# Segment sum of 100,000 edges in a graph layer: accumulating scatters replaced by a counting sort, plain scatters and one-hot products

## What is computed

```python
xn = layernorm(x)
edge_proj = edge_attr @ W_sum + b_sum            # 100000 x 128 by 128 x 256
sum3d = segment_sum(edge_proj, src, 6250)        # the part that the change is about
gnn = xn + z_in[in_deg] + z_out[out_deg] + sigmoid(cent) + sigmoid(vor) + sum3d
x = x + gnn + linear_attention(xn)               # "mix"
x = x + moe_ffn(layernorm(x))                    # 8 experts, top 2, hidden 1024
```

## Time and profile before

| what | us |
|---|---|
| runs of the kernel | 2334.79, 2337.32, 2340.21 (median 2337.32) |
| span of the profiled execution | 2335.5 |
| POOL busy in the 782 accumulating scatters | 1258.5 |
| last of these scatters starts at | 1541.6 |
| last stretch (FFN) begins at about | 1741 |

### The profile page before, as it was taken

How to read it: one execution, slowest core, us unless ns; L and a number is a source line. 1 busy time by engine, 2 the same in 40 slices (tenths; PEclk the granted TensorE clock), 3 DMA queues, 4 the chain that set the end, 5 groups by cost and what they waited for, 6 DMA issues and landing times.

```text
span 2335.5 us, 38410 instructions
## 1 busy us (share of the span) xinstructions
PE 1721.3 (74%) x12869; PEld 1379.6 (59%) x12869; DVE 1450.0 (62%) x3795; ACT 728.8 (31%) x1607; POOL 1545.5 (66%) x1009
## 2 busy tenths in 40 slices
PE   2555545477778777767777677349479999999998
PEld 1333334344445444556666566249378888888887
DVE  2789978777787777233333332139966666666665
ACT  1011111144444444211111111127344444444442
POOL 2888888888888888888888888830023455444442
PEclk9676655579999999778888888669689999999999
DMA  9987777765454445555555555456618989999995
GB/s 304 231 177 176 144 144 159 151 112 69 69 76 70 69 70 70 76 72 86 74 82 75 81 75 75 44 117 201 200 30 253 268 266 276 274 267 278 270 269 159
DMA packets 401456, 348.02 MB, mean 149 GB/s; under 512 B 39303, under 2 KB 323530, under 8 KB 401260
## 3 DMA queue, kind: packets, MB, share of 16 engines
q1 hardware_dynamic: 268492, 266.72, 36.5%
q0 software_dynamic: 132768, 78.84, 29.2%
HBM read 236.69 MB, written 108.76 MB: 148 GB/s over the span
## 4 chain that ended last, share of the span: by engine, by line
PE 35%; POOL 24%; DMA 18%; issue 14%; DVE 7%; ACT 1%; POOLq 0%; SPq 0%; DVEq 0%; ACTq 0%
POOL node_table L1535 24%; DMA node_table<-edge_sums,row_i 18%; PE bank L730 12%; PE bank L744 12%; PE bank L687 2%; DVE hotB L871 2%; PE bank L607 1%; PE bank L482 1%; PE bank L716 1%; PE bank L699 1%; PE bank L701 1%; DVE hotA L868 1%; PE bank L679 1%; PE bank L663 1%; PE bank L672 1%
## 5 line engine op out<-in xcount | busy, mean ns | idle before, releaser
L1535 POOL DMA_INDIRECT node_table<-edge_sums,row_i x782 | 1258.5, 1609 | 278.8 <-issue 207.6
L1333 ACT COPY edge_sums<-bank 128x387 f32<-128x387 f32 (+1 forms) x261 | 125.2, 480 | 1055.1 <-DMA node_table<-edge_sums,row_i 801.8
L482 PE MATMUL bank<-edge_rows,same_node 128*128 128x129 f32 x1564 | 289.9, 333 | 208.7 <-issue 108.0
L482 PEld LDWEIGHTS bank<-edge_rows,same_node 128*128 128x128 f32 x1564 | 248.0, 236 | 254.0 <-issue 230.6
L1561 POOL DMA_INDIRECT result<-mixw,edge_rows x105 | 168.2, 1602 | 283.7 <-DVE mixw L1290 198.4
L1487 ACT ACTIVATE mixw<-bank,edge_rows 128x256 f32<-128x256 f32 (+1 forms) x456 | 243.2, 548 | 328.4 <-PE bank L730 212.7
L730 PE MATMUL bank<-edge_rows,big 128*128 128x256 f16 (+1 forms) x2736 | 290.9, 265 | 4.6 <-ACT mixw L1487 2.3
L744 PE MATMUL bank<-big 128*128 128x256 f16 x2520 | 284.4, 273 | 1.0 <-issue 1.0
L730 PEld LDWEIGHTS bank<-edge_rows,big 128*128 128x128 f16 x2736 | 250.0, 98 | 37.5 <-ACT mixw L1487 3.1
L504 PE MATMUL bank<-hotA,hotB 128*128 128x49 bf16 x1564 | 116.6, 200 | 198.6 <-DVE hotB L871 190.2
L744 PEld LDWEIGHTS bank<-big 128*128 128x128 f16 x2520 | 244.2, 98 | 28.5 <-issue 1.3
(11 more groups left out here) (283 smaller groups left out, 2515.3 us busy)
## 6 DMA issues: line engine op xcount, KB each, us to landing
big<-w_parts SPq DMA_DIRECT2D x114, 1024.0 KB
edge_rows<-edge_attr SPq DMA_DIRECT2D x130, 384.0 KB
big<-L_ffn_W SPq DMA_DIRECT2D x128, 128.0 KB
w_parts<-big SPq DMA_DIRECT2D x64, 256.0 KB
node_table<-z_parts SPq DMA_DIRECT2D x20, 640.0 KB, 7.4
node_table<-edge_sums,row_i POOLq DMA_INDIRECT x782
mixw<-node_table SPq DMA_DIRECT2D x96, 128.0 KB, 2.4
edge_rows<-L_ffn_b SPq DMA_DIRECT2D x57, 128.0 KB
```

The source lines that it names most:

```text
L482: ins = e.matmul(ps_sum[:, i * XW:(i + 1) * XW], S[:, g % SRING, i * P:(i + 1) * P], X[:, c // LOAD % XRING, c % LOAD, :], start=True, sto ...
L1535: e.indirect_dma_start(table[t], bass.IndirectOffsetOnAxis(ap=row_i[:, g % ORING, i:i + 1], axis=0), O[:, g % ORING, i, 0:RW], None, compu ...
```

## The change

The edge rows are no longer added in DRAM. The program finds for each edge its place in the order by node tile (a counting sort over 50 tiles, in four parts of 60, 300, 280 and 142 columns), writes the raw rows with their node number as a 129th value to that place with a plain indirect DMA, reads the sorted rows back in blocks of 256, and sums each block with one-hot products into an accumulator in SBUF (128 x 50 x 128, transposed). A block that holds rows of more than one tile is visited once for each tile: 588 visits in 147 batches of 4. The tables, their zeroing, the matching of equal nodes and the loads of the tables are gone. The degree steps now take 10 columns, and all numbers for one-hots are stored twice side by side, so that the innermost axis of each operand is two adjacent bf16 values. There are 312 ticks, two for each load of 5 columns. The counting of the first 6 chunks and then of all 79 comes ahead of tick 0. In the side steps, ACT's second normalization of `state` is dropped (an identity matrix is added into `mq` instead), and the rest stage turns `xn` again instead of keeping it.

```diff
-GROUP = 3
-LOAD = 6
-TABLES = 4
-START = 8
-TICKS = GROUPS + 5
-DEGREES = 3.6
+LOAD, XRING = 5, 5
+CHUNK = 2 * LOAD
+PART_ENDS = (6, 36, 64, CHUNKS)
+VROWS, VB = 2, 4
+X2RING = 3
+TICKS = 2 * LOADS
+START = 14
+SIDE_AT = ((START, 0), (96, W_TICK0 + W_TICKS), (176, FOLD0), (TICKS - 16, SIDE_STEPS))
+DEGREE_AT = ((START, 0), (136, 2 * CHUNKS + 2))
+VISIT_TICKS = ((100, 0), (4 * PART_ENDS[1], VISIT_AT[1] // VB), (4 * PART_ENDS[2], VISIT_AT[2] // VB),
+               (TICKS, VISIT_AT[3] // VB))
...
+    def tensor_rank(e, k):
...
+        e.matmul(ps_rank_hot[:, 0:w], rankm, sort_hot[:, n % 2, 0:w], start=True, stop=False).then_inc(hot_used, 1)
+        row = identh[:, k:k + 1].to_broadcast([P, P])
+        e.matmul(ps_rank_hot[:, 0:w], row, base_hi[:, 0:w], start=False, stop=False)
+        e.matmul(ps_rank_hot[:, 0:w], row, base_lo[:, 0:w], start=False, stop=True).then_inc(ranked, 1)
...
+    def tensor_visit(e, v):
+        b = v - 3
...
+        for i in range(VB):
+            for k in range(VROWS):
+                ins = e.matmul(ps_visit[b % 2][:, i * P:(i + 1) * P], visit_rows[:, b % X2RING, i, k, 0:EDIM],
+                               visit_hot[:, b % 2, i, k, :], start=(k == 0), stop=(k == VROWS - 1))
+        ins.then_inc(visit_summed, 1)
...
+    def one_hots(out, n, width, values, c0):
+        half = width // 2
+        return (out.rearrange("p (a b r) -> p a b r", a=n, r=2),
+                iotab[:, 0:width].rearrange("p (b r) -> p b r", r=2).unsqueeze(1).to_broadcast([P, n, half, 2]),
+                values[:, c0:c0 + n, :].unsqueeze(2).to_broadcast([P, n, half, 2]))
...
+    def vector_rank(e, k):
...
+        e.reduce_max(sort_top[:, k % 2, 0:n], ps_rank_hot[:, 0:n * SORT].rearrange("p (j g) -> p j g", j=n), AX.X).then_inc(rank_read, 1)
+        e.wait_ge(rank_read, k + 1)
+        e.tensor_scalar(row_pos[:, c0:c0 + n], sort_top[:, k % 2, 0:n], float(PART_FIRST[q] * CHUNK * P) - BIG, None,
+                        ALU.add).then_inc(pos_made, 1)
...
+    def vector_visit(e, v, regs):
+        b = v - 4
+        if 0 <= b < BATCHES:
+            e.load(regs, visit_i[OFF_ROW:OFF_ROW + 1, VB * b:VB * (b + 1)])
+            e.wait_ge(visit_summed, b + 1)
+            for i in range(VB):
...
+                e.tensor_tensor(acc[:, bass.ds(o, P)], acc[:, bass.ds(o, P)], ps_visit[b % 2][:, i * P:(i + 1) * P],
+                                ALU.add).then_inc(acc_added, 1)
+        b = v - 2
+        if 0 <= b < BATCHES:
+            e.wait_ge(visit_loaded[b % X2RING], 16 * VB * (b // X2RING + 1))
...
+            e.tensor_tensor(visit_hot[:, b % 2].rearrange("p v k n -> p (v k) n"), iota.unsqueeze(1).to_broadcast([P, n, P]),
+                            visit_key[:, b % 2].rearrange("p v k -> p (v k)").unsqueeze(2).to_broadcast([P, n, P]),
+                            ALU.is_equal).then_inc(visit_hot_made, 1)
...
+    def scalar_key(e, n):
...
+        x_free(e, n)
+        e.copy(X[:, n % XRING, :, EDIM:XW], src_f[:, c:c + LOAD].unsqueeze(2)).then_inc(keyed, 1)
...
     def scalar_edges(e, tick):
...
+        n, i = divmod(tick, 2)
+        if i == 0 and n >= 2:
+            scalar_key(e, n + XRING - 2)
...
-                e.indirect_dma_start(table[t], bass.IndirectOffsetOnAxis(ap=row_i[:, g % ORING, i:i + 1], axis=0),
-                                     O[:, g % ORING, i, 0:RW], None, compute_op=ALU.add, bounds_check=ROWS - 1,
-                                     oob_is_err=True).then_inc(table_added[t], 16)
...
+    def pool_scatter(e, c, rows, done):
+        e.indirect_dma_start(sorted_rows, bass.IndirectOffsetOnAxis(ap=row_pos[:, c:c + 1], axis=0), rows, None,
+                             bounds_check=ETILES * P - 1, oob_is_err=True).then_inc(done, 16)
...
+    def sync_visit(e, b):
...
+        for q in range(PARTS):
+            if b == VISIT_AT[q] // VB:
+                part_sorted(e, q)
+        if b >= X2RING:
+            e.wait_ge(visit_summed, b - X2RING + 1)
+        for i in range(VB):
+            n = VB * b + i
+            at_ = e.value_load(visit_i[BLOCK_ROW:BLOCK_ROW + 1, n:n + 1], min_val=0, max_val=sum(PART_BLOCKS) - 1)
+            e.dma_start(visit_rows[:, b % X2RING, i].rearrange("p k w -> p (k w)"),
+                        sorted_blocks[bass.ds(at_, 1)].rearrange("o p n -> p (o n)")).then_inc(visit_loaded[b % X2RING], 16)
```

More of the change, by code:

```diff
@@ L188, in build_layer @@
+    wide = scratch(VMAX)
+    ends_f = scratch(2 * P)
+    ends_i = scratch(2 * P).bitcast(I32)
+    ends_b = scratch(2 * P)
+    taken, visit_n, visit_end, visit_at, visit_skip = (scratch(P) for _ in range(5))
+    passed_v, owner_v = scratch(VMAX), scratch(VMAX)
+    upto = scratch(P)
+    assert at[0] <= TILES * DIM
     edge_mem = X.rearrange("p a b c -> p (a b c)")
@@ new lines, in build_layer, with x_there, x_free, part_sorted @@
+    SMALL_ALL = 16 * (KC * 3 + PAIRS + 5 + 4)
+    def x_there(e, n):
+        e.wait_ge(x_loaded[n % XRING], 16 * (n // XRING + 1))
+    def x_free(e, n):
+        if n >= XRING:
+            e.wait_ge(scattered[n % XRING], 16 * LOAD * (n // XRING))
+    def part_sorted(e, q):
+        n = min(LOADS, 2 * PART_ENDS[q])
+        for r in range(XRING):
+            more = ETILES - LOADS * LOAD if q == PARTS - 1 and r == LOADS % XRING else 0
+            e.wait_ge(scattered[r], 16 * (LOAD * len(range(r, n, XRING)) + more))
@@ L758, in tensor_program @@
                 tensor_rest(e, u)
-        for tick in range(TILES + 13):
+        for v in visit_steps(TICKS):
+            tensor_visit(e, v)
+        for tick in range(TILES + 8):
             tensor_nodes(e, tick)
@@ L1306, in vector_program @@
                 vector_rest(e, u)
-        for tick in range(TILES + 13):
+        for v in visit_steps(TICKS):
+            vector_visit(e, v, regs)
+        for tick in range(TILES + 9):
             vector_nodes(e, tick)
@@ L1490, in scalar_program @@
     def scalar_program(e):
-        scalar_index(e)
+        for n in range(XRING):
+            scalar_key(e, n)
         for tick in range(TICKS):
             scalar_edges(e, tick)
+            for v in visit_steps(tick):
+                scalar_visit(e, v)
             for d in degree_steps(tick):
@@ L1539, in pool_gather, with pool_last_edges @@
+    def pool_last_edges(e):
+        e.wait_ge(x_last, 32)
+        e.wait_ge(keyed, LOADS + 1)
+        e.wait_ge(pos_made, CHUNKS)
+        for c in range(LOADS * LOAD, ETILES):
+            pool_scatter(e, c, XL[:, c - LOADS * LOAD, :], scattered[LOADS % XRING])
     def pool_gather(e, j):
@@ L1565, in pool_program @@
         pool_constants(e)
-        for tick in range(TICKS):
-            pool_edges(e, tick)
+        for n in range(LOADS):
+            pool_edges(e, n)
+        pool_last_edges(e)
         for j in range(XG - 1):
@@ L1820, in sync_program @@
             sync_edges(e, tick)
+            for v in visit_steps(tick):
+                sync_visit(e, v)
             for d in degree_steps(tick):
```

815 lines of the change are left out of this document (447 added, 368 removed).

## The result

The changed kernel took 2501.94 us (median of 4 runs), the kernel before 2336.06 beside it: a ratio of 1.070, 95% interval 1.067 to 1.073. Foretold were 2260 us and a gain. The profiled execution took 2489.35 us, its span 2487.6.

The account below looks back on a forecast made before the run. It took POOL's scatter beat to bound most of the edge stage, then DVE the nodes stage. Edge stages at their slowest engine, 1475 us, plus 98.6 and 683.5, gave 2257, stated as 2260; range 2130 to 2370.

Parts of the forecast that it names:

- the tail: From the last scatter to the nodes stage: landing 4 us, 120 visits on SP 137, last batch 10, start 3; 154 us.
- stage by stage, the slowest engine each time: Edge stage: each stage priced by its slowest engine, 100 + 320 + 385 + 285 + 231 + 154 = 1475 us.
- POOL's beat: Plain scatters on POOL: 1.01 us of work plus 0.30 of issue, 1.31 us, against 1.85 with accumulation.
- rival 2: POOL's plain scatter keeps the accumulating scatter's beat of 1.85 us: 2434 us in all; chance 12%.
- One-hots at half rate: DVE's one-hots with paired bf16 operands: 500 wide take 0.42 us, 1280 wide 0.82.
- Rival 3: DVE's one-hots don't run in pairs and take the full rate: 2410 us in all; chance 10%.
- DVE's register reads: Four registers read from SBUF by DVE before each batch of visits: between nothing and 0.75 us, 0.3 taken.
- the 30 us: Ticks 14 to 96: DMA engines might just fill if the new pair stayed as dear; only the range allowed this.
- SP, 1.14 us a visit: Each of 588 visits costs SP a register read and a DMA, 1.14 us; 4.6 us a batch of four.
- POOL beside DVE: Edge stage: the trace does not bear out that DVE's two-SBUF-input instructions delay POOL's scatters; 1% chance left.
- rival 1: POOL stays the bound in the ticks because the other engines overlap better: about 2035 us; chance 8%.

Follow-up runs that it names:

- e13: The changed kernel unchanged, run again in a later job: 2222.6 us, ratio 0.954 to the kernel before.
- e14: The changed kernel with SP reading a batch's four block numbers in one load of four registers: 2131.9 us, ratio 0.915 to the kernel before.
- e11: The changed kernel with POOL clearing a 320-wide scratch tile after each scatter, beat 1.53 us: 2307.1 us, ratio 0.989 to the kernel before.
- e12: The changed kernel with POOL's 320-wide clear after each scatter and SP's one load of four registers per batch: 2232.7 us, ratio 0.957 to the kernel before.
- e5: The changed kernel unchanged, run once more beside the kernel before: 2510.4 us, ratio 1.075.
- e10: The changed kernel unchanged, run beside two paused variants in one job: 2460.5 us, ratio 1.054 to the kernel before.
- e3: The changed kernel without the visits (block loads, keys, one-hots, products, adds), so edge sums stay zero: 1939.8 us.
- e4: The changed kernel with SP loading the visits' blocks from constant addresses, without the 588 register reads: 2118.4 us.

## Why the prediction was wrong

**Its sum came out within 2% where signals were prompt, in part by luck.** In e13 none was late, and the stages can be set against the working (the first four: DVE's maximum L1032 in ticks 14, 98, 178 and 258; the prediction's points shifted by its own rate for two ticks):

| until | foretold | e13 | first profile |
|---|---|---|---|
| tick 14 | 100 | 114 | 161 |
| tick 98 | 430 | 414 | 506 |
| tick 178 | 812 | 784 | 949 |
| tick 258 | 1098 | 1054 | 1289 |
| last scatter | 1321 | 1270 | 1531 |
| nodes stage begins | 1475 | 1451 | 1715 |
| end (span) | 2257 | 2223 | 2488 |

Against e13 the ticks were priced 51 us too dear up to the last scatter and the tail 27 too cheap, and the two errors hide one another. The first profile loses to e13 47, 45, 73, 70 and 26 us up to the last scatter and 3 in the tail, where POOL is silent; nodes, router and FFN take 772 us in both. That is, it loses where POOL scatters the edges and nowhere else.

**The step that failed** is the sentence that sums "stage by stage, the slowest engine each time". It takes for granted that each engine learns at once when PE is done, as all rows of before have it, and it prices POOL's faster beat as a gain only. The runs showed in its place: at a beat of 1.29 us PE's signals come late, by up to 22.8 us, in four of the seven jobs of the changed kernel and its variants; engines that take turns with PE wait, and a stage takes longer than any engine's work in it. No row of before has that; its beat is 1.85. The size is shown twice: 279 us between the first measurement and e13, across jobs, and 153 us within one job when the pauses are put in. The range's upper end of 2370 held 110 us for dearer DMAs, dearer register reads and some waits for PE. A lesson for the range: the change took POOL and the DMAs that it starts to a rate that no row showed, and the rows then set no bound on what the other engines suffer by it.

The windows tell it for the mix stage, the first of e13, the second of the first profile:

```profile
379.00:785.00 406.00, 342.81 (x2053) 220.31 (x2052) 284.04 (x648) 166.57 (x392) 261.03 (x238) 0.95 0.47 129
```

```profile
450.00:922.00 472.00, 352.58 (x1974) 218.42 (x1973) 272.61 (x615) 163.66 (x384) 233.49 (x220) 0.88 0.37 102
```

In e13 PE is busy 84% at a clock share of 0.95, and the 49 tiles take 393 us, about as foretold (47 of them in 385). That agreement is partly luck: the sum had 362 us of work for PE in 385, the window has 343 in 406. In the first profile the 49 tiles take 475 us, with PE 75% busy and its clock at 0.88.

Point by point:
- **POOL's beat** 0.98 + 0.30 = 1.28 us: right (1.31 from the gather), and rival 2's fixed price is out. 521 of the 781 beats of e13 are of this length; others wait or are stretched (see the end). That accumulation is dear by its third descriptor no trace shows.
- **One-hots at half rate**: 500 wide 0.41 us, 1280 wide 0.82: right. Rival 3 did not come.
- **DVE's register reads**: 0.3 was taken; in the first profile and in e13 0.41 us of issue (median) stand ahead of a batch's first add where nothing else ends the wait.
- **DMA bandwidth**: the 30 us weren't needed. Ticks 14 to 98 take 300 us in e13, where 330 were foretold; in the window of 120 to 379 us the DMA engines are busy 0.73.
- **SP, 1.14 us a visit**: right. In e13's tail the visits go at 1.10 to 1.32; PE's 572 products in 160 us are 35.8 batches of 16, 4.47 us each, against 4.6. SP's chain in this tail (L1868 is the DMA's issue, L1867 the read of one register), and the window:

```profile
1300.92 0.34 SPq L1868
1301.30 0.27 SPq L1867
1301.60 0.15 SPq L1867
...
1302.02 0.34 SPq L1868
```

```profile
1280.00:1440.00 160.00, 97.66 (x572) 89.10 (x571) 86.01 (x212) 0.00 (x0) 0.00 (x0) 0.78 0.44 118
```

- **The tail**: 181 us instead of 154. The price was right and the number not: 622 products, 39 batches, come behind the last scatter, not 30: visits of the third part were still to be loaded or in flight. With one read for four numbers (e14) it is 109. Two DMAs of a batch then start 0.53 apart, and DVE is the bound, busy 82% and waited for by PE, as its 3.0 us a batch would have it: 31 batches in 90 us are 2.9 each. SP's chain and the window in e14:

```profile
1299.95 0.33 SPq L1868
...
1300.48 0.33 SPq L1868
...
1301.00 1.11 SPq L1868
```

```profile
1260.00:1350.00 90.00, 63.24 (x495) 57.33 (x494) 73.49 (x186) 0.00 (x0) 0.00 (x0) 1.00 0.67 185
```

- **POOL beside DVE**: "the trace does not bear it out" was misread. In the earlier trace rows a scatter takes 82.67 / 51 = 1.62 us with DVE busy 88.5 of 100, 83.88 / 53 = 1.58 at 80.8 and 83.54 / 55 = 1.52 at 33.4. The last section has what it is worth.
- **Slips in the sums**: 782 x 1.31 is 1024 and not 1028; rival 1 then adds up to 2026, and rival 2 to 2432; 60 pairs and 16 matchings leave 38 us of the 88.5 and not 36; 362 and 268 us at a clock of 0.95 are 381 and 282. None changes the verdict.
- **The chances**: I gave 23% to slower, with two causes, rivals 2 and 3, neither of which came. A mechanism that no row hints at had no chance of its own.

## What to carry to other kernels

A wait that ends long after its producer did, several waiters of one engine let go at the same moment, and a producer whose next instructions run on undisturbed point at a late signal and not at a slow engine. A lacking record alone doesn't: DVE's had no effect here. Count late signals by comparing the raise of the semaphore with the end of the instruction, and lacking records beside them, before pricing anything else. A verdict on a change that raises the rate of POOL's indirect DMAs needs the unchanged partner in the same job, and more than one job; and the cheapest test is a pause behind each DMA. Where addresses for several DMAs lie side by side, read them with one load of several registers: 72 us of tail here from e13 to e14, 76 from e11 to e12, and 91 and 74 us in all.

## What the runs showed that was not expected

- **PE's signals, and not DVE's or ACT's, arrive late** in some jobs while POOL issues indirect DMAs 1.29 us apart: 262 to 289 of 787 to 941 recorded in the first measurement and e5 to e10; 32 of 960 at 1.53; none of 1507 at 1.85 in the kernel before. In e3, e4, e13 and e14 none was late at the same 1.29. The jobs differ in the records that lack; what makes them differ the traces don't show, nor why it is PE.
- **The scatters themselves wait for some of DVE's instructions.** In e13 their median is 0.98 us and their mean 1.12; the excess over 0.98 sums to 113 us. What counts is what DVE is at when the scatter starts. Of 96 that start during the one-hot L1071, whose inputs both lie in SBUF, 76 take over 1.1 us, and all but one of these end 0.85 to 0.86 us after the one-hot. Of 100 that start during the adds L1059, with one input in PSUM, none does; beside an idle DVE 1 of 226. A scatter that was there before L1071 isn't stretched (0 of 68). Two scatters of e13 and the one-hot that holds the second (645.91 + 1.22 + 0.85 = 647.98):

```profile
645.19 0.98 POOL L1760 DMA_INDIRECT sorted_rows<-edge_rows,sorted_pos  x1 [0.30 <-issue]
...
645.91 1.22 DVE L1071 TENSOR_TENSOR big<-iota,big 128x1024 f32<-128x1024 f32 x1
...
646.47 1.51 POOL L1760 DMA_INDIRECT sorted_rows<-edge_rows,sorted_pos  x1 [0.30 <-issue]
```

The Trainium skill, "SBUF — State Buffer", Who interferes with whom, says that a DVE instruction with two SBUF inputs and a GpSimd instruction that reads SBUF contend, and that one lock decides it. The trace bears this out for POOL, which waits where DVE was first. For DVE it shows no wait: L1071 takes 1.22 to 1.30 us in either order. The kernel before has it too: of 133 scatters that start during its one-hot L871, with both inputs in SBUF, 79 are over 0.12 us longer than the usual 1.55, beside an idle DVE 1 of 341. It did not decide here: in e13 PE and SP were the bound.
